# Self attention of a decoder: the subtracted maxima copied into the score banks by ScalarE, and the weighted sums issued in four pieces per group

## The chip, the cores and the metric

The kernel runs on one core of one Trainium2 chip. The metric is the device time of the whole program in microseconds (us), over several runs; the median is given. One further execution was recorded by the hardware profiler, and every row below is from that one. PE is TensorE's matmul, PEld its load of the stationary operand, DVE is VectorE, ACT is ScalarE, POOL is GpSimd.

## The reference, cut to what matters

The program is a two-layer decoder on `x` of shape (8, 512, 256). The change touches one of its six stages, the self attention of the second layer, which comes after a feed-forward stage and before a cross attention:

```
qkv = X @ W_qkv                              # X: layernorm of x; 16 heads of 64
scores = einsum('bqhd,bkhd->bhqk', q, k) / sqrt(64)
weights = softmax(scores, axis=-1)
attn = einsum('bhqk,bkhd->bqhd', weights, v)
x = x + attn.reshape(b, s, h * d) @ W_out
```

There are 8 batch elements of 512 tokens. All is float32.

## The kernel before, in words

Scores are held transposed, keys on the partitions and queries along the free axis, so that the product with V needs no transpose. Two heads (2 x 64 = 128 rows) make a **group**; a batch element has 8 groups, c = 0 to 7, and a group has 4 **chunks** of 128 keys, k = 0 to 3. For a chunk, "exact" (L1588, L1591) computes the two heads' scores, 128 keys x 512 queries each, into the two banks of the PSUM tensor ST. float32 precision is reached by splitting q and k into a high and a low part: three products per head (high-high, high-low, low-high), and in the kernel before a fourth (L1591) that multiplies a row of ones with `mrow`, the negated maximum of every query, and so subtracts the maximum from the scores. ScalarE then takes the exponential of both banks at once (L1649) into `PT`. There is one ST, so the next chunk's scores wait for this exponential.

The maxima come from a pass ahead of it. "max" (L1568) computes rough scores of one block of 128 queries, with queries on the partitions, into SM; VectorE reduces them (L1671) into `nmax`. When a group's four reductions are done, "mt" (L1575) transposes `nmax` with four small matmuls into one bank of W, and ScalarE copies that to `mrow` (L1644). `nmax` is 128 columns wide per block, with zeros where no maximum stands.

The other work of the stage: "q", "k", "v" and "norm" (L1535, L1546) are the projections and transposed activations, three groups and more ahead of their use. "av" (L1601) multiplies all four chunks of `PT` with V into OP, 16 instructions in one run; ScalarE copies the result out (L1653). "sum" (L1608) multiplies ones with `U`, the sum of a group's four chunks of `PT` that GpSimd makes (L1709, L1712), and so gives the softmax's denominators; VectorE takes their reciprocal (L1685) and scales the result (L1688). "out" (L1616) is the last projection.

Every engine walks the same list, which the function `plan` writes out by hand, and takes from it the steps that are its own, strictly in that order. A step that waits holds up everything behind it on its engine. In a middle group TensorE's order is: exact 0, max, q; exact 1, max, k; exact 2, max, sum (of the group before); exact 3, mt, v; av; max.

The steps q, k, v, norm, mt, sum and out share the three banks of W in rotation: each takes the bank that the third-last such step had, and waits (`free_bank`) until its reader has released it. ScalarE releases the banks of v and mt. VectorE releases the others, that of sum when the reciprocal ends. In a middle group the rotation before is q, k, sum, mt, v.

The last batch element has its own list, without the steps that prepare a next one. The rest run in a loop of seven passes.

## Time and profile before

| | |
|---|---|
| median of 3 runs | 3023.49 us (3019.45 to 3025.32) |
| the profiled execution: its own time | 3020.66 us |
| its span, first to last instruction | 3018.8 us |
| PE busy over the span | 91% |
| DVE, ACT, POOL busy over the span | 64%, 48%, 37% |

The span is the part of the profiled execution that the trace covers; 1.9 us lie around it. Busy shares are means over six stages with different limits. The self attention runs from about 1050 to 2196 us after the span's start, one batch element every 144.3 us.

### The profile page before, as it was taken

Reading aid. Unit: us, or ns where it says so; the run is one execution under the profiler, and the core shown is the slowest. Engines: PE = TensorE matmul, PEld = TensorE weight load, DVE = VectorE, ACT = ScalarE, POOL = GpSimd, SP = SyncE. Lnnn points to the kernel's source line nnn. Section 1 sums busy time; section 2 is a strip of 40 time slices with the busy share of each in tenths; the row PEclk is TensorE's granted clock in tenths of the full one; section 3 lists DMA queues with packets and bytes.
Section 4 is the critical chain, followed back from the end, with each engine's and each line's share of the span. In section 5 each row is a group of like instructions: output and inputs, shape, how many; then the busy total and the mean of one; then the engine's idle time right before and its main releaser. Section 6 shows DMA issues by size and latency. Waiting matters only on the chain. (4 is left out here: it accounts for less than half of the span.)

```text
span 3018.8 us, 49274 instructions
## 1 busy us (share of the span) xinstructions
PE 2760.4 (91%) x16604; PEld 1622.9 (54%) x16605; DVE 1922.6 (64%) x3109; ACT 1446.6 (48%) x2224; POOL 1103.7 (37%) x853
## 2 busy tenths in 40 slices
PE   7997899999868899999999999999889999966998
PEld 4774333333335555555555555555445555566997
DVE  5775666667668766657575757575645555474565
ACT  2342566666668743434343434343335555543333
POOL 3233332222037243434343434343443333153333
PEclk9998899999979999999999999999989999958999
DMA  5002222222111000000000000000043222146665
GB/s 159 0 0 74 53 58 56 57 57 52 33 56 43 1 1 1 0 0 0 0 0 0 0 0 0 0 0 0 1 110 79 71 67 71 45 113 232 214 218 194
DMA packets 102928, 159.71 MB, mean 53 GB/s; under 512 B 28349, under 2 KB 63432, under 8 KB 97160
## 3 DMA queue, kind: packets, MB, share of 16 engines
q1 hardware_dynamic: 97784, 147.88, 17.0%
q0 software_dynamic: 3408, 8.46, 0.8%
q10 hardware_dynamic: 1600, 1.61, 0.2%
q8 instruction: 79, 1.29, 0.2%
q14 instruction: 57, 0.47, 0.1%
HBM read 91.79 MB, written 14.96 MB: 35 GB/s over the span
## 5 line engine op out<-in xcount | busy, mean ns | idle before, releaser
L1671 DVE TENSOR_REDUCE self_nmax<-self_SM 128x2 f32<-128x1024 f32 x256 | 313.8, 1226 | 185.3 <-PE self_SM L1568 178.5
L522 DVE TENSOR_REDUCE cross_nmax<-cross_S 128x2 f32<-128x1024 f32 x256 | 311.7, 1224 | 153.3 <-PE cross_S L347 152.4
L1709 POOL TENSOR_TENSOR self_U<-self_PT 128x1024 f32<-128x1024 f32 x64 | 153.1, 2392 | 626.0 <-ACT self_PT L1649 626.0
L1649 ACT ACTIVATE self_PT<-self_ST 128x1024 f32<-128x1024 f32 x256 | 262.3, 1025 | 217.1 <-PE self_ST L1591 217.1
L1712 POOL TENSOR_TENSOR self_U<-self_U,self_PT 128x1024 f32<-128x1024 f32 x128 | 304.0, 2375 | 55.2 <-ACT self_PT L1649 50.7
L456 ACT ACTIVATE cross_PT<-cross_S 128x1024 f32<-128x1024 f32 x256 | 260.7, 1025 | 118.0 <-PE cross_S L358 117.1
L1186 DVE TENSOR_REDUCE cross_nmax<-cross_S 128x4 f32<-128x1024 f32 x128 | 156.7, 1224 | 143.3 <-PE cross_S L984 143.1
L1601 PE MATMUL self_OP<-self_PT,self_V 128*64 128x512 f32 x1024 | 233.8, 598 | 10.0 <-ACT self_PT L1649 10.0
L1685 DVE RECIPROCAL self_rcp<-self_W 128x512 f32<-128x512 f32 x64 | 214.1, 3345 | 8.4 <-PE self_W L1608 8.4
L1112 ACT ACTIVATE cross_PT<-cross_S 128x1024 f32<-128x1024 f32 x128 | 131.0, 1023 | 121.4 <-PE cross_S L1000 121.4
L377 PE MATMUL cross_W<-cross_PT,cross_V 128*32 128x512 f32 x1024 | 139.1, 618 | 8.0 <-DVE cross_rsin L554 8.0
L1601 PEld LDWEIGHTS self_OP<-self_PT,self_V 128*64 128x64 f32 x1024 | 69.5, 136 | 139.1 <-issue 132.8
L358 PEld LDWEIGHTS cross_S<-cross_qs,cross_ks 51*128 51x128 f32 x512 | 48.3, 186 | 169.9 <-issue 120.5
L617 POOL TENSOR_TENSOR cross_rows<-cross_rows,cross_cos 128x512 f32<-128x512 f32 x30 | 38.4, 1280 | 276.6 <-DVE cross_rsin L554 276.6
L1588 PE MATMUL self_ST<-self_q_hi,self_k_hi 64*128 64x512 f32 x512 | 123.0, 476 | 16.6 <-ACT self_PT L1649 15.4
L358 PE MATMUL cross_S<-cross_qs,cross_ks 51*128 51x512 f32 x512 | 129.4, 504 | 6.9 <-DMA cross_qs<-cross_mrow 3.3
L1653 ACT COPY self_Oraw<-self_OP 128x512 f32<-128x512 f32 x64 | 37.5, 587 | 197.2 <-PE self_OP L1601 197.2
L1568 PE MATMUL self_SM<-self_k_hi,self_q_hi 64*128 64x512 f32 x512 | 114.0, 440 | 19.2 <-DVE self_nmax L1671 19.2
L347 PE MATMUL cross_S<-cross_ks,cross_qs 49*128 49x512 f32 x512 | 109.3, 424 | 12.6 <-ACT cross_PT L456 11.1
L3100 PE MATMUL moe_TR<-moe_W,moe_hid_hi 128*128 x312 | 114.8, 406 | 0.0
L1616 PE MATMUL self_W<-self_wo,self_OT 128*128 128x256 f32 x512 | 112.5, 380 | 1.0 <-DVE self_OT L1688 1.0
L1588 PEld LDWEIGHTS self_ST<-self_q_hi,self_k_hi 64*128 64x128 f32 x512 | 47.8, 183 | 119.4 <-ACT self_PT L1649 70.1
(435 smaller groups left out, 6401.8 us busy)
## 6 DMA issues: line engine op xcount, KB each, us to landing
moe_staged<-in_L_ffn_W SPq DMA_DIRECT2D x36, 1024.0 KB, 5.9
cross_ks<-cross_parts SPq DMA_DIRECT2D x384, 64.0 KB, 2.2
cross_qs<-cross_parts SPq DMA_DIRECT2D x376, 64.0 KB, 2.3
all_x<-in_L_ffn_W SPq DMA_DIRECT2D x14, 1024.0 KB
all_x<-sorted_rows SPq DMA_DIRECT2D x83, 130.0 KB, 2.3
cross_cT<-in_ctx_T SPq DMA_DIRECT2D x16, 512.0 KB, 4.3
sorted_rows<-all_spare_row SPq DMA_DIRECT2D x1, 5460.0 KB, 23.8
all_x<-in_x SPq DMA_DIRECT2D x8, 512.0 KB, 6.1
```

What stands on the lines that cost most here:

```text
L358: m = pe.matmul(dst[:, r, :], ks[rows_r, p, k * P:(k + 1) * P], qs[rows_r, p, :], start=True, stop=True)
L377: m = pe.matmul(dst[32 * j:32 * j + 32, :], V[:, b % 2, k, 2 * p + r, :], PT[:, pt_slot[("exact", b, NT * p + k)], r, :], start=(k == 0), ...
L456: act.activation(PT[:, pt_slot[st], :, :], S[:, slot[st], :, :], ACT.Exp).then_inc(s_exped, 1)
L522: dve.tensor_reduce(nmax[:, g % 2, 0:R, n % PER_G], S[:, slot[st], :, :], AX.X, ALU.max, negate=True).then_inc(s_maxed, 1)
L1186: dve.tensor_reduce(nmax[:, g % 2, 0:R, n0:n0 + 2], S[:, slot[st], :, :].rearrange("p r (i c) -> p r i c", i=2), AX.X, ALU.max, negate=Tru ...
L1588: pe.matmul(ST[:, j, :], l[at, slot, at_k], r[at, slot, :], start=(t == 0), stop=False)
L1601: m = pe.matmul(OP[j * D:(j + 1) * D, :], V[:, k, 2 * n + j, :], PT[:, k, j, :], start=(k == 0), stop=(k == NT - 1), skip_group_check=True)
L1649: act.activation(PT[:, k, :, :], ST[:, :, :], ACT.Exp).then_inc(exped.sem, 1)
L1671: dve.tensor_reduce(nmax[:, i, 0:P:D], SM[:, :, :], AX.X, ALU.max, negate=True).then_inc(maxed.sem, 1)
L1685: dve.reciprocal(rcp[:, :], bank_of(order, st)).then_inc(done, 1)
L1709: pool.tensor_tensor(U[:, c % 2, :, :], PT[:, 0, :, :], PT[:, 1, :, :], ALU.add).then_inc(added.sem, 1)
L1712: pool.tensor_tensor(U[:, c % 2, :, :], U[:, c % 2, :, :], PT[:, k, :, :], ALU.add).then_inc(added.sem, 1)
```

## The change

In the score banks: the product of ones with `mrow` is gone. ScalarE writes the negated maxima into ST before the chunk's scores are computed, and the three remaining products of every chunk add onto them. For that "mt" becomes two steps per group, one for each head: four transposes of a maximum column that is broadcast along the free axis, so that the bank then holds the negated maxima of all 512 queries on every partition. ScalarE copies such a bank twice, into ST (for chunk 0 of the next group) and into a new SBUF tensor `least`. For chunks 1 to 3 it copies `least` to ST (128 x 1024) after the exponential of the chunk before. A new counter, `filled`, tells TensorE that the banks are ready. Two matmuls at the very start of the stage write ST once.

In the weighted sums: "av" becomes four steps of 4 instructions, one per chunk. The piece of chunk k - 1 comes after the other work behind exact k; the last piece of a group comes in the next group, behind exact 0 and q. Group 7 issues its last piece itself, before its own sum.

Two memsets by GpSimd in the stage before are gone.

```diff
@@ -1372,7 +1372,7 @@
         self.low = [s.sb(n, [P, KC, H * 64], F32R) for n in ("wq_lo", "wk_lo", "wv_lo")]
         self.wo = s.sb("wo", [P, H * 64 // P, C])
         self.hT_hi, self.hT_lo = s.sb("hT_hi", [P, KC, T], F32R), s.sb("hT_lo", [P, KC, T], F32R)
-        self.nmax, self.ones_r, self.ones = s.sb("nmax", [P, NT, P]), s.sb("ones_r", [P, P], F32R), s.sb("ones", [P, 64])
+        self.nmax, self.ones = s.sb("nmax", [P, NT, 2]), s.sb("ones", [P, 64])
         self.half, self.eps, self.minus = (s.sb(n, [P, NT]) for n in ("half", "eps", "minus"))
 
 
@@ -1406,6 +1406,9 @@
                 add("exact", c * NT + k, NC * NT)
                 if k < NT - 1:
                     add("max", (c + 1) * NT + k + 1, NC * NT)
+                else:
+                    for j in range(2):
+                        add("mt", (c + 1) * 2 + j, NC * 2)
                 if k == 0:
                     add("q", c + 2, NC)
                 elif k == 1:
@@ -1420,16 +1423,17 @@
                     if c:
                         add("sum", c - 1, NC)
                 else:
-                    add("mt", c + 1, NC)
                     if c < NT:
                         add("v", NT + c, HALF * NT)
                     if c == 5:
                         add("norm", KC + 1, KC)
                     if c >= 6:
                         add("v", HALF * NT + 2 * (c - 6), HALF * NT)
-            add("av", c, NC)
+                if k or c:
+                    add("av", c * NT + k - 1, NC * NT)
             add("max", (c + 2) * NT, NC * NT)
             if c == NC - 1:
+                add("av", NC * NT - 1, NC * NT)
                 add("sum", c, NC)
             if c >= 6:
                 add("v", HALF * NT + 2 * (c - 6) + 1, HALF * NT)
@@ -1446,7 +1450,7 @@
                "act": lambda kind: kind in RINGED and drained_by(kind) == "act",
                "dve": lambda kind: kind in RINGED and drained_by(kind) == "dve",
                "split": lambda kind: kind in ("q", "k", "norm")}
-    for kind in ("exact", "max", "av", "sum"):
+    for kind in ("exact", "max", "sum"):
         counted[kind] = lambda k, kind=kind: k == kind
 
     class Pass:
@@ -1471,10 +1475,10 @@
         s = Space(nc, ctx, "self1")
         h_tok = x_mem[:, 0:NT, :]
         (wq, wk, wv), (wq_lo, wk_lo, wv_lo), wo = buffers.high, buffers.low, buffers.wo
-        hT_hi, hT_lo, nmax, ones_r, ones = buffers.hT_hi, buffers.hT_lo, buffers.nmax, buffers.ones_r, buffers.ones
+        hT_hi, hT_lo, nmax, ones = buffers.hT_hi, buffers.hT_lo, buffers.nmax, buffers.ones
         half, eps, minus = buffers.half, buffers.eps, buffers.minus
         q_hi, q_lo, k_hi, k_lo = (s.sb(n, [P, SLOTS_QK, T], F32R) for n in ("q_hi", "q_lo", "k_hi", "k_lo"))
-        mrow = s.sb("mrow", [P, T], F32R)
+        least = s.sb("least", [P, 2, T])
         V = s.sb("V", [P, NT, H, D])
         PT = s.sb("PT", [P, NT, 2, T])
         U = s.sb("U", [P, 2, 2, T])
@@ -1496,7 +1500,8 @@
         split = loop("split", "split")
         scored, exped = loop("scored", "exact"), loop("exped", "exact")
         guarded, maxed = loop("guarded", "max"), loop("maxed", "max")
-        valued, lifted = loop("valued", "av"), loop("lifted", "av")
+        valued, lifted = Loop(s.sem("valued"), NC), Loop(s.sem("lifted"), NC)
+        filled = Loop(s.sem("filled"), NC * (NT + 1), 2)
         scaled = loop("scaled", "sum")
         added = Loop(s.sem("added"), 3 * NC)
         normed, s_stat, rooted = Loop(s.sem("normed"), NT), Loop(s.sem("stat"), 2 * NT), Loop(s.sem("rooted"), 4)
@@ -1536,7 +1541,7 @@
             return m
 
         def tensor_steps(pe, b, order):
-            n_exact = n_max = 0
+            n_max = 0
             for st in order.steps:
                 kind, n, rel = st
                 if kind == "norm":
@@ -1569,38 +1574,38 @@
                                       start=True, stop=True)
                     m.then_inc(guarded.sem, 1)
                 elif kind == "mt":
+                    c, j = n // 2, n % 2
                     dst = free_bank(pe, b, order, st)
-                    reach(pe, maxed, "max", b, order, ("max", n * NT + NT - 1, rel))
+                    if j == 0:
+                        reach(pe, maxed, "max", b, order, ("max", c * NT + NT - 1, rel))
                     for i in range(NT):
-                        m = pe.transpose(dst[:, i * P:(i + 1) * P], nmax[:, i, :], ident)
+                        m = pe.transpose(dst[:, i * P:(i + 1) * P], nmax[:, i, j:j + 1].to_broadcast([P, P]), ident)
                     m.then_inc(ring_full.sem, 1)
                 elif kind == "exact":
                     c, k = n // NT, n % NT
-                    exped.wait(pe, b, n_exact)
-                    n_exact += 1
+                    filled.wait(pe, b, (NT + 1) * c + k)
                     if k == 0:
                         reach(pe, drained["dve"], "dve", b, order, ("k", c, rel))
-                        reach(pe, drained["act"], "act", b, order, ("mt", c, rel))
                     slot, at_k = c % SLOTS_QK, slice(k * P, (k + 1) * P)
                     for t, (l, r) in enumerate(((k_hi, q_hi), (k_hi, q_lo), (k_lo, q_hi))):
                         for j in range(2):
                             at = slice(j * D, (j + 1) * D)
-                            pe.matmul(ST[:, j, :], l[at, slot, at_k], r[at, slot, :], start=(t == 0), stop=False)
-                    for j in range(2):
-                        at = slice(j * D, (j + 1) * D)
-                        m = pe.matmul(ST[:, j, :], ones_r[at, :], mrow[at, :], start=False, stop=True)
+                            m = pe.matmul(ST[:, j, :], l[at, slot, at_k], r[at, slot, :], start=False, stop=(t == 2),
+                                          skip_group_check=True)
                     m.then_inc(scored.sem, 1)
                 elif kind == "av":
-                    exped.wait(pe, b, NT * (n + 1))
-                    lifted.wait(pe, b, n)
-                    if n in (0, NC // 2):
-                        v = n // (NC // 2)
-                        reach(pe, drained["act"], "act", b, order, ("v", v * NT + NT - 1, rel))
-                    for k in range(NT):
-                        for j in range(2):
-                            m = pe.matmul(OP[j * D:(j + 1) * D, :], V[:, k, 2 * n + j, :], PT[:, k, j, :],
-                                          start=(k == 0), stop=(k == NT - 1), skip_group_check=True)
-                    m.then_inc(valued.sem, 1)
+                    c, k = n // NT, n % NT
+                    exped.wait(pe, b, n + 1)
+                    if k == 0:
+                        lifted.wait(pe, b, c)
+                        if c in (0, NC // 2):
+                            v = c // (NC // 2)
+                            reach(pe, drained["act"], "act", b, order, ("v", v * NT + NT - 1, rel))
+                    for j in range(2):
+                        m = pe.matmul(OP[j * D:(j + 1) * D, :], V[:, k, 2 * c + j, :], PT[:, k, j, :],
+                                      start=(k == 0), stop=(k == NT - 1), skip_group_check=True)
+                    if k == NT - 1:
+                        m.then_inc(valued.sem, 1)
                 elif kind == "sum":
                     dst = free_bank(pe, b, order, st)
                     added.wait(pe, b, 3 * (n + 1))
@@ -1641,16 +1646,26 @@
                     v, i = n // NT, n % NT
                     act.copy(V[:, i, v * 8:(v + 1) * 8, :], src.rearrange("p (h d) -> p h d", d=D)).then_inc(drained["act"].sem, 1)
                 elif kind == "mt":
-                    act.copy(mrow[:, :], src).then_inc(drained["act"].sem, 1)
+                    c, j = n // 2, n % 2
+                    exped.wait(act, b, 0 if order is first else NT * (NC if rel else c))
+                    act.copy(ST[:, j, :], src).then_inc(filled.sem, 1)
+                    filled.wait(act, b, 0 if order is first else (NT + 1) * ((NC if rel else c) - 1) + NT - 1)
+                    act.copy(least[:, j, :], src).then_inc(drained["act"].sem, 1)
                 elif kind == "exact":
                     c, k = n // NT, n % NT
                     scored.wait(act, b, n + 1)
                     added.wait(act, b, 3 * (c - 1) + max(k, 1))
                     act.activation(PT[:, k, :, :], ST[:, :, :], ACT.Exp).then_inc(exped.sem, 1)
-                elif kind == "av":
-                    valued.wait(act, b, n + 1)
-                    scaled.wait(act, b, n - 1)
-                    act.copy(Oraw[:, n % 2, :], OP[:, :]).then_inc(lifted.sem, 1)
+                    if k < NT - 1:
+                        if k == 0:
+                            reach(act, drained["act"], "act", b, order, ("mt", 2 * c + 1, rel))
+                        exped.wait(act, b, n + 1)
+                        act.copy(ST[:, :, :], least[:, :, :]).then_inc(filled.sem, 1)
+                elif kind == "av" and n % NT == NT - 1:
+                    c = n // NT
+                    valued.wait(act, b, c + 1)
+                    scaled.wait(act, b, c - 1)
+                    act.copy(Oraw[:, c % 2, :], OP[:, :]).then_inc(lifted.sem, 1)
 
         def vector_steps(dve, b, order):
             n_max = 0
@@ -1668,7 +1683,7 @@
                     c, i = n // NT, n % NT
                     n_max += 1
                     guarded.wait(dve, b, n_max)
-                    dve.tensor_reduce(nmax[:, i, 0:P:D], SM[:, :, :], AX.X, ALU.max, negate=True).then_inc(maxed.sem, 1)
+                    dve.tensor_reduce(nmax[:, i, :], SM[:, :, :], AX.X, ALU.max, negate=True).then_inc(maxed.sem, 1)
                 elif kind in ("q", "k", "norm"):
                     split.wait(dve, b, order.nth["split"][st])
                     src = bank_of(order, st)
@@ -1714,6 +1729,8 @@
         with nc.Block() as block:
             @block.tensor
             def _(pe):
+                for j in range(2):
+                    pe.matmul(ST[:, j, :], wq[:, 0, 0:P], hT_hi[:, 0, :], start=True, stop=True)
                 tensor_steps(pe, None, first)
                 for counter in (ring_full, scored, guarded, valued):
                     counter.credit(pe)
@@ -1724,7 +1741,7 @@
             @block.scalar
             def _(act):
                 scalar_steps(act, None, first)
-                for counter in (drained["act"], split, exped, lifted, normed):
+                for counter in (drained["act"], split, exped, filled, lifted, normed):
                     counter.credit(act)
                 with act.Fori(0, B - 1) as b:
                     scalar_steps(act, b, whole)
@@ -2595,8 +2612,6 @@
                 bound_x(1)
                 for tensor, value in ((following.half, -0.5), (following.eps, EPS), (following.minus, -1.0), (following.ones, 1.0)):
                     pool.memset(tensor[:, :], value).then_inc(s_fset, 1)
-                pool.memset(following.ones_r[:, :].bitcast(F32), 1.0).then_inc(s_fset, 1)
-                pool.memset(following.nmax[:, :, :], 0.0).then_inc(s_fset, 1)
                 normalise(1, range(NT))
                 for t in range(TILES + 1):
                     b, i = t // NT, t % NT
```

## Rows read from the trace of the kernel before

In a row of a stretch stand: start and end, its length, the busy time and count of PE, PEld, DVE, ACT and POOL, the granted clock of PE, the DMA share and GB/s.

**Rows 1.** Stretches: groups 0, 1, 4, 5, 6, 7 and one batch element.

```profile
1484.45:1500.49 16.04, 14.43 (x80) 8.16 (x80) 5.48 (x6) 7.67 (x10) 7.14 (x3) 1.00 0.00 0
1500.49:1516.35 15.86, 15.47 (x84) 8.30 (x82) 11.35 (x8) 6.93 (x10) 7.17 (x3) 1.00 0.00 0
...
1548.13:1563.48 15.35, 14.17 (x78) 7.46 (x76) 11.39 (x8) 6.35 (x9) 7.11 (x3) 1.00 0.00 0
1563.48:1579.29 15.81, 15.17 (x86) 8.12 (x84) 12.27 (x10) 7.30 (x11) 7.12 (x3) 1.00 0.00 0
1579.29:1596.87 17.58, 17.19 (x90) 9.19 (x87) 12.57 (x9) 7.30 (x10) 7.15 (x3) 1.00 0.00 0
1596.87:1628.73 31.86, 31.86 (x157) 21.56 (x156) 16.57 (x13) 8.10 (x11) 7.15 (x3) 1.00 0.00 0
1484.45:1628.73 144.28, 139.29 (x729) 79.34 (x728) 94.28 (x78) 59.37 (x79) 58.68 (x28) 1.00 0.00 0
```

**Rows 2.** Timeline of PE, group 1: start us, duration, operation, count [idle before].

```profile
1500.15 0.51 PE L1568 MATMUL self_SM<-self_k_hi,self_q_hi 64*128 64x512 f32 x2
1500.49 0.40 PE L1588 MATMUL self_ST<-self_q_hi,self_k_hi 64*128 64x512 f32 x2
...
1501.18 0.40 PE L1591 MATMUL self_ST<-self_mrow,self_ones_r 64*128 64x512 f32 x2
1501.97 0.50 PE L1568 MATMUL self_SM<-self_k_hi,self_q_hi 64*128 64x512 f32 x2 [0.39 <-DVE self_nmax L1671]
1502.40 0.50 PE L1535 MATMUL self_W<-self_hT_hi,self_wq 128*128 128x512 f32 x1
...
1503.98 0.51 PE L1588 MATMUL self_ST<-self_q_hi,self_k_hi 64*128 64x512 f32 x2
...
1508.30 1.08 PE L1608 MATMUL self_W<-self_U,self_ones 128*64 128x512 f32 x4
1509.33 0.50 PE L1588 MATMUL self_ST<-self_q_hi,self_k_hi 64*128 64x512 f32 x2
...
1510.46 0.66 PE L1575 MATMUL self_W<-all_ident,self_nmax 128*128 128x128 f32 x4
1510.87 0.47 PE L1535 MATMUL self_W<-self_wv,self_hT_hi 128*128 128x512 f32 x1
...
1512.43 3.65 PE L1601 MATMUL self_OP<-self_PT,self_V 128*64 128x512 f32 x16
1516.02 0.50 PE L1568 MATMUL self_SM<-self_k_hi,self_q_hi 64*128 64x512 f32 x2
```

**Rows 3.** Timeline of DVE, group 1: the last reduction, the reciprocal, the scaling.

```profile
1508.41 1.23 DVE L1671 TENSOR_REDUCE self_nmax<-self_SM 128x2 f32<-128x1024 f32 x1
1509.56 3.35 DVE L1685 RECIPROCAL self_rcp<-self_W 128x512 f32<-128x512 f32 x1
1513.03 1.81 DVE L1688 TENSOR_TENSOR self_OT<-self_Oraw,self_rcp 128x512 f32<-128x512 f32 x1
```

**Rows 4.** Timeline of ACT, end of group 1: an exponential and the copy behind it.

```profile
1510.65 1.03 ACT L1649 ACTIVATE self_PT<-self_ST 128x1024 f32<-128x1024 f32 x1 [1.37 <-PE self_ST L1591]
1511.58 0.58 ACT L1644 CAST self_mrow<-self_W 128x512 fp32r<-128x512 f32 x1
```

**Rows 5.** Timeline of PE, last group: a chunk's last product, the next chunk's first.

```profile
2170.45 0.40 PE L1591 MATMUL self_ST<-self_mrow,self_ones_r 64*128 64x512 f32 x2
2171.96 0.50 PE L1588 MATMUL self_ST<-self_q_hi,self_k_hi 64*128 64x512 f32 x2 [1.11 <-ACT self_PT L1649]
```

**Rows 6.** Timeline of DVE, group 5: norm's low part, ahead of the reciprocal.

```profile
1572.81 0.69 DVE L1681 TENSOR_TENSOR self_hT_lo<-self_W,self_hT_hi 128x512 fp32r<-128x512 f32 x1
```

**Rows 7.** Timeline of PE: the first matmul after the stage's end.

```profile
2203.65 1.97 PE L1062 MATMUL cross_W<-all_ident,all_x 128*128 128x128 f32 x8 [7.28 <-ACT all_x L1129]
```

**Rows 8.** Stretches behind that matmul; columns as in rows 1.

```profile
2206.00:2208.00 2.00, 2.00 (x4) 0.70 (x3) 0.00 (x0) 0.24 (x1) 0.00 (x0) 0.50 0.90 314
...
2210.00:2214.00 4.00, 4.00 (x13) 2.20 (x12) 2.33 (x4) 0.69 (x1) 2.26 (x2) 1.00 0.19 47
```

## The prediction

> **What bounds the kernel now.** I read the page's shares first: PE is busy 91% of the span, no other engine above 64%. Then the stretches of the stage [rows 1]: a batch element takes 144.28 us, PE is busy in 139.29 of them at a granted clock of 1.00 (2.4 GHz), and ACT works 59. TensorE's own list therefore sets the pace. Its waits in the timeline of a middle group are one, of 0.39, on a reduction [rows 2]. So an edit counts by what it does to TensorE's start-to-start times, and by the waits it creates there.
>
> Those times come from the timeline of PE [rows 2]. One exact after max takes 0.34 to the next start in front and 0.23 for each further pair of products: the fourth product starts at 1501.18, 0.69 after the first (0.23 a pair). max to exact is 0.34. q from its start to exact is 1.58 (1502.40 to 1503.98). sum, 4 instructions, is 1.03 from start to next start. exact 3 to mt is 1.13, mt to v 0.41, v to av 1.56, and av, 16 instructions, 3.59 (1512.43 to 1516.02). The wait on the reduction makes two maxes stand at least 1.82 apart (1500.15 to 1501.97).
>
> **Work of TensorE, per group.** The product of ones goes: 4 x 0.23 = -0.92. The second mt: +0.41. av in four pieces: a piece has the shape of sum (64 stationary columns, 512 moving ones, 4 instructions), so each costs up to 1.03, four 4.12 in place of 3.59. Behind sum the piece finds the array in the same form; four bare instructions are (3.59 - 0.17) / 4 = 0.86, with 0.17 the excess of sum over this, so one piece is about 0.86 and the others 1.03. I take 1.03 for the piece and 0.86 for the sum ahead of it: 3.95, or +0.36. Both maxes around exact 0 still stand 1.82 apart, so there exact's 0.23 turns into wait: +0.23. Together -0.92 + 0.41 + 0.36 + 0.23 = +0.08: the saving is already spent. Counted alone, the product of ones would be worth 256 x 0.23 = 59 us; the other three terms take that back.
>
> **The cycle of ST.** From a chunk's last product to the next chunk's first it now takes 1.51 (2170.45 to 2171.96) where only the exponential stands between [rows 5]. The fill comes on top. No row shows ScalarE writing PSUM. The nearest are the exponential of as many elements, 1.03, and the 512-wide copy, 0.58 [rows 4]. Below: 2 x 0.58 less a fixed part, about 0.9; above: I allow 1.4. I take 1.02 plus 0.05 for waiting on its own exponential, since back-to-back instructions overlap by 0.10 [rows 4] and this one cannot. So 2.58 to 2.60 from last product to next first. The Trainium skill (ScalarE: Activation LUTs, "Step-by-step: what each stage is for") holds that ScalarE writes PSUM faster than SBUF; by that the fill would be at the lower end and the sum some 2 us smaller, and no row here shows it.
>
> **The bank rotation.** The rotation of W becomes q, k, sum, mt, mt, v. The third-last step before v is now sum (it was k), and sum's bank is freed only when the reciprocal ends. The reciprocal starts 1.26 after sum and takes 3.35 [rows 2, 3]. So v can't start before sum + 4.66, whereas before it started at sum + 2.57 while the reciprocal ran. This is what decides.
>
> **A middle group walked through** (exact 0 at 0, in us). max 1.48, q 1.91, av piece 3.49, exact 1 at 4.52 (ST ready at 3.1, hidden). max 5.32, k 5.65, av piece 7.24, exact 2 at 8.27 (ST ready 7.7, hidden). max 9.07, sum 9.40, av piece 10.26, done 11.29. ST is ready at 8.84 + 2.60 = 11.44: exact 3 waits 0.15. mt 12.34, second mt 12.75, v could go at 13.16, but its bank is free at 9.40 + 4.66 = 14.06: 0.90 of wait. v to 15.62, av piece to 16.65, max to 16.99. ScalarE's four copies after exact 3 (ST, least, ST, least) have ST ready by 15.1: hidden. GpSimd's three sums need 7.2 of 17: hidden, and so is the copy out of OP. Group: 16.99 against 15.86 [rows 1], +1.13. A fill slower by 0.7 changes little here, since v's wait takes it up.
>
> The page on TensorE of the Trainium skill (TensorE: Matmul & The Clock Gate, "Part 4: PE-mode transpose") gives about 275 ns for a transpose in a kernel. The timeline has four of them in 0.41 from start to start, so they overlap; four of 275 ns would be 1.1, and the sum about 30 us larger.
>
> **The other groups, same method.** Group 0 has no sum before its v and no av piece behind exact 0. Exact 1 waits for the exponential and the fill (0.74 later than before, as the fill is longer than the product of ones it replaces), exact 3 for the fill: 15.99 against 16.04, -0.05. Group 4 has no v: the next exact 0 waits for the second mt's fill, 15.1 against 15.35, -0.2. Group 5: its second norm takes the bank of sum. There the reciprocal is later too, for VectorE must first make norm's low part, 0.69 [rows 6], and that waits for ScalarE's high part, now queued behind exponential and fill (until 12.5 after exact 0). Also the reduction of group 4's last max waits for the scaling, up to 1.81 long [rows 3] and behind the late reciprocal, +0.47. Reciprocal 13.1 to 16.45, norm at 16.5 (waits 2.4), group 18.46 against 15.81: +2.65. Group 6: as a middle one, 19.07 against 17.58, +1.5. Group 7 has five av pieces and v behind a reciprocal, 33.55 against 31.86, +1.7; out hides its last reciprocal as before. Sum: -0.05 + 3 x 1.1 - 0.2 + 2.65 + 1.5 + 1.7 = +8.9 per batch element, 62 for seven. The last element, with no norm and no v at its end, I put at +5. The second mt and its copies at the entry: +0.4. The two removed memsets lie on GpSimd in a stage where PE doesn't wait for them: 0.
>
> **Sum.** 3020.66 + 62 + 5 + 0.4 = 3088. The median shown is 2.8 above the profiled execution, so 3090 on that scale.
>
> **Rivals.**
> *The bank of sum costs nothing* (I misread the rotation, or the reciprocal is out of the way earlier). Five groups lose their 0.90, group 5 its 2.4: 6.9 x 7 and 2.7, or 51 less, 3039. For it: nothing but possible error; the reciprocal has never been under 3.3 in a row. 6%.
> *Faster*: v does not wait, and a piece of av costs the bare 0.86. Then a group is -0.92 + 0.41 - 0.15 + 0.23 = -0.43, 64 of them -27: 2996. It decides only if both hold: without the bank's wait the break-even is a piece of 0.97, with it 0.65, under the four bare instructions. Against it: the 1.03 of sum in the same place. 3%.
> *The clock falls* in the new gaps. After PE stood idle for 7.28 us its next matmuls ran at 0.50 (1.2 GHz), until some point from 2208 to 2210, and at 1.00 later [rows 7, 8]; after gaps of 1.1 it stayed at 1.00. Group 5's wait of 2.4 lies between. 5 us at half speed lose 2.5, seven times: 17 more, 3107. 8%. The Trainium skill's page on TensorE ("HAM oscillation") also has idle gaps between bursts bring the slower clock.
> *The fill is dear* (1.4): groups 0, 4 and 7 lose 3 x 0.4, others 0.2: 12 more, 3102. 10%.
>
> **Chances and range.** Forecast 70%, its own range 3075 to 3103 (a piece of 0.86 everywhere takes 3 x 0.17 per v group off, about 15; fill at either end -2 to +12). Dear fill 10%, clock 8%, free bank 6%, faster 3%, other 3%. I leave out free bank and faster below and take in the clock above: 3055 to 3115. Faster 4%, same (within 0.2%, about 6 us, which is what a measurement of this kernel can tell from none) 2%, slower 94%.
>
> **What would show it.** In the profile after: v (L1535 after the second mt) waits about 0.9 for the DVE reciprocal in groups 1 to 3, 6, 7, norm in group 5 about 2.4; a middle group lasts 17.0; L1601 runs as pieces of 4 at 1.03; exact 3 waits 0.1 to 0.2 for ScalarE; the granted clock stays 1.00. Wrong would be: no wait on the reciprocal, a fill far from 1.02, or ScalarE named as the releaser in most waits.

## The result, and the profile after

| | before | after |
|---|---|---|
| median of 4 runs each | 3022.14 us (3019.45 to 3025.32) | 3115.02 us (3111.2 to 3119.66) |
| profiled execution, its span | 3020.66, 3018.8 | 3111.2, 3109.4 |
| mean of the seven batch elements in the loop | 144.28 | 157.02 |

The changed kernel is slower by 3.1% (ratio 1.0308, 95% interval 1.029 to 1.0326). The forecast was 3090 with a range of 3055 to 3115: the sign was right, the size 25 us too small, and the median lies 0.02 us above the upper end. Nearly all of it lies in the loop: 7 x (157.02 - 144.28) = 89.2 of the 90.5 us between the two profiled executions. The last element is 6.1 longer, and what lies ahead of and behind the stage 4.8 shorter.

The page of the changed kernel, its busy times and two groups:

```profile
PE 2772.9 (89%) x16350; PEld 1593.5 (51%) x16351; DVE 1935.0 (62%) x3109; ACT 1740.4 (56%) x2608; POOL 1105.8 (36%) x851
...
L1605 PE MATMUL self_OP<-self_PT,self_V 128*64 128x512 f32 x1024 | 277.7, 621 | 0.1
...
L1663 ACT COPY self_ST<-self_least 128x1024 f32<-128x1024 f32 x192 | 195.4, 1018 | 9.6
```

The fill takes 1018 ns (I had taken 1.02 us). ScalarE is at 56%, far from a bound. PE's share fell from 91% to 89%, so it now waits more.

The stretches of the changed kernel, groups 0 to 7 of the fourth batch element and the element as a whole (columns as in [rows 1]):

```profile
1519.20:1535.34 16.14, 13.35 (x71) 7.37 (x72) 5.49 (x6) 11.93 (x15) 7.11 (x3) 1.00 0.00 1
1535.34:1552.30 16.96, 15.58 (x80) 7.75 (x78) 12.02 (x8) 11.64 (x16) 7.13 (x3) 1.00 0.00 0
1552.30:1571.07 18.77, 15.59 (x80) 7.77 (x78) 12.79 (x16) 11.52 (x15) 8.66 (x7) 1.00 0.00 0
1571.07:1588.00 16.93, 15.57 (x80) 7.77 (x78) 10.24 (x8) 13.31 (x19) 7.32 (x3) 1.00 0.00 0
1588.00:1603.17 15.17, 14.09 (x75) 6.62 (x72) 10.73 (x8) 10.47 (x14) 6.38 (x4) 1.00 0.00 0
1603.17:1622.46 19.29, 15.62 (x80) 7.88 (x82) 13.26 (x11) 12.49 (x17) 7.92 (x4) 0.97 0.00 0
1622.46:1642.99 20.53, 19.75 (x87) 9.95 (x83) 13.32 (x9) 11.49 (x15) 7.13 (x3) 0.86 0.00 0
1642.99:1676.50 33.51, 32.76 (x158) 21.45 (x157) 17.71 (x13) 13.10 (x18) 7.14 (x3) 1.00 0.00 1
1519.20:1676.50 157.30, 142.33 (x698) 76.58 (x697) 95.55 (x78) 95.94 (x127) 58.78 (x28) 0.98 0.00 0
```

Three things are to be seen. Groups 1, 3, 4 and 7 are within 0.07 of what the prediction walked through (16.99, 16.99, 15.1, 33.55; "the walk" from here on). Group 2 has the same PE work as group 1 (15.59 busy against 15.58) and yet takes 1.81 longer: a wait that the walk does not have. In groups 5 and 6 the granted clock stands at 0.97 and 0.86, where it was 1.00 before [rows 1].

The PE timeline of group 1 (columns as in [rows 2]) shows the wait that was forecast:

```profile
1544.70 1.08 PE L1613 MATMUL self_W<-self_U,self_ones 128*64 128x512 f32 x4
1545.61 1.03 PE L1605 MATMUL self_OP<-self_PT,self_V 128*64 128x512 f32 x4
1546.71 0.50 PE L1593 MATMUL self_ST<-self_q_hi,self_k_hi 64*128 64x512 f32 x2
1547.60 1.09 PE L1582 MATMUL self_W<-all_ident,self_nmax 128*128 128x128 f32 x8
1549.36 0.50 PE L1540 MATMUL self_W<-self_wv,self_hT_hi 128*128 128x512 f32 x1 [0.67 <-DVE self_rcp L1700]
1550.96 1.08 PE L1605 MATMUL self_OP<-self_PT,self_V 128*64 128x512 f32 x4
```

The time from sum to v is 4.66 (1544.70 to 1549.36), to the hundredth what the walk had: the reciprocal starts 1.26 after sum, takes 3.35, and v starts 0.05 behind its end. (The prediction's text names only the first two, 4.61.) sum and the piece behind it take 0.91 and 1.10 to the next start, together 2.01 (1.89 was assumed, and 0.15 of wait). The idle time in brackets, 0.67, looks less than the 0.90 forecast, but it is counted from an end that the profile models. From start to start the eight transposes take 0.84 where nothing holds v up (group 0, 1531.59 to 1532.43) and 1.76 here: the wait costs 0.92. In group 2 the same wait has 2.49 of idle. The DVE timeline of that group says why:

```profile
1562.91 1.40 DVE L1677 BATCH_NORM_STATS2 self_stats<-all_x 128x6 f32 x4
1564.46 0.38 DVE L1681 BATCH_NORM_AGGREGATE self_mv<-self_stats 128x2 f32<-128x6 f32 x4 [0.16 <-DVE self_stats L1677]
1564.76 3.33 DVE L1700 RECIPROCAL self_rcp<-self_W 128x512 f32<-128x512 f32 x1
```

Eight small instructions of the layernorm statistics ("stat" in the list, for the next batch element) stand ahead of the reciprocal: 1.85 us from 1562.91 to 1564.76. They stood there before as well, as the same view of the kernel before shows:

```profile
1525.43 1.40 DVE L1662 BATCH_NORM_STATS2 self_stats<-all_x 128x6 f32 x4
1526.98 0.38 DVE L1666 BATCH_NORM_AGGREGATE self_mv<-self_stats 128x2 f32<-128x6 f32 x4 [0.16 <-DVE self_stats L1662]
1527.28 3.32 DVE L1685 RECIPROCAL self_rcp<-self_W 128x512 f32<-128x512 f32 x1
```

There the group's sum starts at 1524.17, so its reciprocal comes 3.11 behind it and not 1.26 as in group 1. That cost TensorE nothing while v took the bank of k. Since sum's bank is now the one that v needs, every microsecond ahead of the reciprocal is one of TensorE's.

The releasers of PE's waits in the changed kernel (total us, times, longest):

```profile
PE self_W L1540 <- DVE self_rcp L1700: 37.1, 38, 2.5
PE self_SM L1573 <- DVE self_nmax L1686: 36.1, 44, 1.6
...
PE self_ST L1593 <- ACT self_ST L1663: 24.4, 20, 1.8
...
PE self_W L1551 <- DVE self_rcp L1700: 14.5, 7, 2.1
```

The first and the last line are the bank's wait, 51.6 in all; the wait on the reductions was there before, at 19.2.

And the clock, in the PE timeline at the end of group 5 and the start of group 6:

```profile
1620.09 0.66 PE L1551 MATMUL self_W<-all_ident,all_x 128*128 128x128 f32 x4 [2.06 <-DVE self_rcp L1700]
...
1625.31 0.63 PE L1540 MATMUL self_W<-self_hT_lo,self_wq 128*128 128x512 f32 x1
1625.73 0.63 PE L1540 MATMUL self_W<-self_hT_hi,self_wq_lo 128*128 128x512 f32 x1
```

Products that follow each other at 0.23 elsewhere are 0.42 apart here. The time at half clock can be read from the stretches as 2 x (1 - granted clock) x length, summed over the groups: 3.4 to 7.0 us in each of the seven batch elements, in groups 5 and 6 and in three of the seven also in group 2 (which is then 20.1 to 20.2 long).

### The profile page after: what moved, and what is told of

Its sections match the earlier page's. It is cut to its first block and busy times, and to the rows that moved or that the text cites. A ratio compares the mean times of both kernels' runs of the same rounds, so it can differ in the third digit from the quotient of the medians.

```text
span 3109.4 us, 49675 instructions
## 1 busy us (share of the span) xinstructions
PE 2772.9 (89%) x16350; PEld 1593.5 (51%) x16351; DVE 1935.0 (62%) x3109; ACT 1740.4 (56%) x2608; POOL 1105.8 (36%) x851
## 3 DMA queue, kind: packets, MB, share of 16 engines
q10 hardware_dynamic: 1600, 1.61, 0.2%
## 5 line engine op out<-in xcount | busy, mean ns | idle before, releaser
L1605 PE MATMUL self_OP<-self_PT,self_V 128*64 128x512 f32 x1024 | 277.7, 621 | 0.1
L1186 DVE TENSOR_REDUCE cross_nmax<-cross_S 128x4 f32<-128x1024 f32 x128 | 156.8, 1225 | 141.7 <-PE cross_S L984 141.5
L1663 ACT COPY self_ST<-self_least 128x1024 f32<-128x1024 f32 x192 | 195.4, 1018 | 9.6
L1112 ACT ACTIVATE cross_PT<-cross_S 128x1024 f32<-128x1024 f32 x128 | 131.1, 1024 | 119.7 <-PE cross_S L1000 119.7
L1593 PE MATMUL self_ST<-self_q_hi,self_k_hi 64*128 64x512 f32 x512 | 125.4, 486 | 33.8 <-ACT self_ST L1663 24.4
L1703 DVE TENSOR_TENSOR self_OT<-self_Oraw,self_rcp 128x512 f32<-128x512 f32 x64 | 118.8, 1856 | 6.5
```

The source lines that it names most:

```text
L1186: dve.tensor_reduce(nmax[:, g % 2, 0:R, n0:n0 + 2], S[:, slot[st], :, :].rearrange("p r (i c) -> p r i c", i=2), AX.X, ALU.max, negate=Tru ...
L1593: m = pe.matmul(ST[:, j, :], l[at, slot, at_k], r[at, slot, :], start=False, stop=(t == 2), skip_group_check=True)
L1605: m = pe.matmul(OP[j * D:(j + 1) * D, :], V[:, k, 2 * c + j, :], PT[:, k, j, :], start=(k == 0), stop=(k == NT - 1), skip_group_check=True)
L1663: act.copy(ST[:, :, :], least[:, :, :]).then_inc(filled.sem, 1)
```

## The experiments

Each ratio is against the kernel before, run on the same chip beside it. Where a difference is small, the stage itself says more than the whole time. In the sixteen profiled executions its first scores start between 1048.3 and 1056.2 us, and what lies behind it takes 819 to 827, with no order by kernel. So the eight batch elements ("the stage" below) are compared as well: 1144.7 us in the kernel before, 1240.1 in the changed one.

| kernel | median us | ratio (95% interval) |
|---|---|---|
| e1, pieces alone | 3105.25 | 1.0277 (1.0258 to 1.0296) |
| e2, maxima alone | 3202.37 | 1.0605 (1.0585 to 1.0625) |
| e3, v ahead of mt | 3080.02 | 1.019 (1.0173 to 1.0207) |
| e4, every fill twice | 3188.84 | 1.0555 (1.0536 to 1.0574) |
| e5, stat behind sum | 3110.44 | 1.0295 (1.0268 to 1.0323) |
| e6, group 5's norms behind av | 3131.34 | 1.0363 (1.0332 to 1.0393) |
| e7, pieces, scaling later | 3021.57 | 0.9993 (0.9981 to 1.0004) |
| e8, all moves | 3005.72 | 0.9943 (0.9921 to 0.9965) |
| e9, scaling later alone | 3098.32 | 1.0245 (1.0228 to 1.0262) |
| e10, before with max ahead of av | 2996.66 | 0.991 (0.9893 to 0.9926) |
| e11, e7 with max ahead | 3004.49 | 0.9928 (0.9911 to 0.9945) |
| e12, e8 with v in group 0 | 2993.32 | 0.9894 (0.9877 to 0.9911) |
| e13, PE kept busy in two waits | 3113.85 | 1.0312 (1.0294 to 1.033) |
| e14, three moves | 3050.47 | 1.0099 (1.0082 to 1.0117) |

### e1 and e2: the two halves of the change alone

e1 is the kernel before, with its product of ones, and the four pieces; e2 is the changed kernel with the weighted sums in one run again. Of e1's edit only the list is shown; the rest is as in the change.

```diff
+                if k or c:
+                    add("av", c * NT + k - 1, NC * NT)
-            add("av", c, NC)
             add("max", (c + 2) * NT, NC * NT)
             if c == NC - 1:
+                add("av", NC * NT - 1, NC * NT)
                 add("sum", c, NC)
...
```

> The kernel before with the weighted sums in four pieces and nothing else. Theory (the pieces cost TensorE its change of form, 32 pieces of 1.03 in place of 8 runs of 3.59, and give back waits for the exponential that they now cover): per batch element 31.8 against 28.7, so +3.1, less the waits covered in groups 0 (0.96), 4 (0.80) and 5 (0.25): +1.1, about +8 in all, 3030 us (3022 to 3040). Rival (the pieces are what made the changed kernel slower): +50 or more, above 3070.

> The changed kernel with the weighted sum again as one run per group behind v. Theory (the fill by ScalarE lengthens the cycle of the score banks to 2.6 us from last product to next, and only the pieces cover it): exact 2 waits 0.45, exact 3 about 1.0, group 0 more; a middle group about 17.9 us against 16.96 in the changed kernel; in all about 3175 us (3150 to 3200). Rival (the pieces are a cost in this kernel too): below 3115.

e2 came close to its expectation, 3202 for 3175, 2 above its range: the fill, no longer covered by a piece of av, is exposed, and PE waits 97.6 us for it in all. e1 did not: 3105, where 3030 was expected. The DVE and POOL timelines of e1, group 1, at its end:

```profile
1541.37 3.35 DVE L1690 RECIPROCAL self_rcp<-self_W 128x512 f32<-128x512 f32 x1
1544.84 2.58 DVE L1693 TENSOR_TENSOR self_OT<-self_Oraw,self_rcp 128x512 f32<-128x512 f32 x1
1547.34 1.21 DVE L1676 TENSOR_REDUCE self_nmax<-self_SM 128x2 f32<-128x1024 f32 x1
```

```profile
1544.49 2.38 POOL L1717 TENSOR_TENSOR self_U<-self_U,self_PT 128x1024 f32<-128x1024 f32 x1 [0.87 <-ACT self_PT L1653]
```

With av spread out, the group's last max comes about two pieces earlier, and VectorE reaches its reduction only after reciprocal and scaling. The scaling itself is stretched from 0.69 to 2.58 while GpSimd adds. The next max then waits, and e1's list of waits has it in one line:

```profile
PE self_SM L1570 <- DVE self_nmax L1676: 75.0, 48, 2.6
```

These 75 us, where the kernel before had 19.2, and the falls of the clock behind them are most of the loss. So the two halves, +82 and +179, do not add up to the +93 of both. The pieces cover the fill. And the group's last max comes later behind the sum than in e1, so that its reduction is less in the way: the wait is 0.63 behind groups 1 and 2 of the changed kernel, and 1.07 and 2.0 behind groups 1 and 2 of e1. The second mt is enough for that, since the wait is still 0.62 behind group 1 of e3 below, where v waits for nothing.

### e3: v ahead of mt

```diff
-                else:
-                    for j in range(2):
-                        add("mt", (c + 1) * 2 + j, NC * 2)
...
                     if c < NT:
                         add("v", NT + c, HALF * NT)
-                    if c == 5:
-                        add("norm", KC + 1, KC)
                     if c >= 6:
                         add("v", HALF * NT + 2 * (c - 6), HALF * NT)
+                    for j in range(2):
+                        add("mt", (c + 1) * 2 + j, NC * 2)
+                    if c == 5:
+                        add("norm", KC + 1, KC)
```

v then takes the bank of k, and mt that of sum only one step later. This is the direct test of the bank rotation.

> The changed kernel with v ahead of the two mt steps, so that the second mt, not v, takes the bank of sum, 4.9 us after sum. Theory (the bank that the reciprocal holds for 4.66 us is what v waits for): the waits of 0.67 in groups 1, 3, 6 and 7 vanish, that of group 2 shrinks from 2.5 to 1.6; 3.6 per batch element, 27 in all: 3088 us (3080 to 3100). Rival (VectorE or ScalarE is the bound and the wait only moves to another step): 3105 to 3120.

3080.02, where 3088 was expected. The line of v's wait on the reciprocal is gone from the list of waits. The norm's 14.5 remains, and a new line has the second mt wait for the reciprocal, 9.9 in all: 1.4 in group 2 of each element, where stat delays it. Groups 1 and 3 are 16.05 and 16.3 for 16.96 and 16.94. By this run the bank of sum in front of v is worth 35 us of the loss. An element without a fall of the clock takes 150.7 here and 154.95 in the changed kernel, which is 30 us for seven, and half of what is left of the 35 is fewer falls. The 27 expected were added up from idle times of 0.67; group 1 became shorter by 0.90, the wait from start to start.

### e4: every fill twice

```diff
                         act.copy(ST[:, :, :], least[:, :, :]).then_inc(filled.sem, 1)
+                        filled.wait(act, b, 2 * NT * c + 2 * k + 1)
+                        act.copy(ST[:, :, :], least[:, :, :]).then_inc(filled.sem, 1)
```

> The changed kernel with every fill of ST from least made twice, one after the other: 192 more copies of 1.02 us and a wait of 0.05 on ScalarE. Theory (the fill is mostly hidden; exact 2 has 0.5 of slack, exact 3 none, and the wait on the reciprocal takes up 0.7): a middle group +0.9, group 0 +2.4 to 3, others 1 to 1.5, about 10 per batch element, 80 in all: 3195 us (3165 to 3225). Rival 1 (the fill is fully exposed, ScalarE bounds the stage): 3 x 1.07 per group, 64 groups, +205: 3320. Rival 2 (the fill is free): 3115.

3188.84 (3195 was expected), or 74 more than the changed kernel, for 192 fills of 1.02 (196 us): between free and fully exposed. Middle groups grow from 16.96 to 17.53, and the wait for ST from 24.4 to 122.9 in total. The single fill is just covered in middle groups, as the walk had it, with little to spare.

### e5, e6 and e9: the three instructions in VectorE's way

e5 moves stat behind sum; e6 moves both norms of group 5 behind the last piece of av in that group; e9 leaves TensorE's list alone and lets VectorE scale one group later.

```diff
-                    if c == 2:
-                        add("stat", 1, 1)
...
                     if c:
                         add("sum", c - 1, NC)
+                    if c == 2:
+                        add("stat", 1, 1)
```

```diff
-                    if c == 5:
-                        add("norm", KC, KC)
...
-                    if c == 5:
-                        add("norm", KC + 1, KC)
...
+            if c == 5:
+                for n in range(KC):
+                    add("norm", KC + n, KC)
             add("max", (c + 2) * NT, NC * NT)
```

```diff
                 if k == 0:
                     add("q", c + 2, NC)
+                    if c >= 2:
+                        add("scale", c - 2, NC)
...
-                    drained["dve"].wait(dve, b, order.nth["dve"][st])
+                elif kind == "scale":
+                    drained["dve"].wait(dve, b, order.nth["dve"][("sum", n, rel)])
                     lifted.wait(dve, b, n + 1)
```

> The changed kernel with VectorE's statistics of the next batch element (group 2, 1.85 us) behind the sum step in place of ahead of it. Theory (they hold back group 2's reciprocal, and with it the bank that v waits for): group 2 from 18.76 to 16.96, seven times 12.6, and the clock falls that followed its wait of 2.5 us in three of seven batch elements, 4 more: 3098 us (3093 to 3104). Rival (something else in group 2): 3112 to 3118.

> The changed kernel with both norm steps of group 5 behind its third av piece, so that neither waits for the reciprocal. Theory (the wait of 2.1 us there costs itself, and once more by the clock that falls behind it, some 1.5 us a time): groups 5 and 6 together from 38.3 to 39.9 down to 35 to 37, seven times 2.5 to 3, 3095 us (3088 to 3102), and a granted clock of 1.00 in group 6. Rival (the clock falls for another reason): groups 5 and 6 lose only the wait and the clock in group 6 stays under 1.00: above 3102.

> The changed kernel with only the scaling of the output moved to the next group's chunk 0. Theory (here, unlike in the kernel with the pieces alone, v's wait on the reciprocal holds the group's last max back far enough that the scaling is done, except behind group 4, which has no v): only group 5's first wait of 1.6 shrinks to about 0.6, seven times 1.0, and a part of the clock falls: 3105 us (3095 to 3112). Rival (the scaling is what costs in this kernel too): below 3060.

e5 gave 3110.44, 5 less than the changed kernel in place of the 17 expected, and the intervals of the two overlap. But e5's stage started 5.8 later and what lies behind it took 3.2 longer, which the edit does not touch; its loop is 11.4 shorter than the changed kernel's. The stretches of e5, groups 2 and 5 of one element, show why it worked and why it did not bring all that was expected:

```profile
1554.72:1571.65 16.93, 15.56 (x80) 7.75 (x78) 11.93 (x16) 11.51 (x15) 4.95 (x3) 1.00 0.00 0
...
1603.80:1624.44 20.64, 16.97 (x80) 8.73 (x82) 13.24 (x11) 12.48 (x17) 7.93 (x4) 0.90 0.00 0
```

Group 2 fell to 16.93 in all seven elements, as it should; group 5 has more time at the lower clock. One of e5's seven elements, the one without a fall, is at 153.04 against the walk's 153.2; their mean is 155.4. So stat is the missing step of the walk. The 4 us expected on top from fewer falls did not come: the clock costs 2.4 per element here, and 2.1 in the changed kernel.

e6 missed: 3131.34, slower by 16 than the changed kernel where 20 less was expected. Groups 5 and 6 take 18.3 and 21.8 in most elements, with a clock of 0.91 and 0.92. The norms' low parts now stood, with the scaling, ahead of the next reduction; the bank's wait had turned into waits of up to 2.4 for the reduction. In the stage the clock fell 23 times, against 10 in the changed kernel.

e9 gave 3098.32 (3105 was expected, below 3060 if the scaling were the cost here too). Group 5 shrinks from 18.87 at full clock to 17.24: its first max had waited 1.61 for group 4's last reduction, which stood behind the scaling, and that wait is gone. The norm's wait of 2.1 stays. Three of its seven elements have no fall, at 153.2 to 153.3.

### e7: pieces alone, scaling later

The edit of e9 on e1.

> The kernel before with the weighted sums in four pieces, as e1, and VectorE's scaling of the output (L1688) moved from right behind the reciprocal to the next group's chunk 0. Theory (in e1 the max at the group's end comes two pieces nearer to the sum, while the reciprocal and the scaling, stretched to 2.5 us while GpSimd adds, still hold VectorE; the next max waits 1.07 to 2.0 and the clock falls behind the longer ones): the wait shrinks to 0.4, the granted clock is 1.00 throughout, 3030 us (3022 to 3045). Rival (the pieces themselves cost 80 us on TensorE): above 3080.

3021.57, the same as the kernel before within its interval, and just under the 3022 to 3045 expected. The DVE timeline has the scaling at its short length, in GpSimd's pause, and the stretch of one element is at 144.58 with a clock of 1.00:

```profile
1540.28 0.68 DVE L1698 TENSOR_TENSOR self_OT<-self_Oraw,self_rcp 128x512 f32<-128x512 f32 x1
```

```profile
1488.62:1633.20 144.58, 141.32 (x730) 77.51 (x730) 86.05 (x78) 59.55 (x79) 58.61 (x28) 1.00 0.00 0
```

The 84 us of e1 were thus the place of one VectorE instruction. The pieces' own TensorE work costs a middle group some 0.3 (16.16 against 15.9), and group 0, which has only three of them, gives 1.56 back (14.48 against 16.04).

### e8, e10, e11 and e12: is there a version that beats both?

e8 is the changed kernel with the moves of e3, e5, e6 and e9, and the group's last max ahead of the piece of av. e10 is the kernel before with that last move alone, e11 is e7 with it, and e12 is e8 with group 0's v put behind its q, where the wait for ST was. Two cuts of these edits follow: the early max, as e10 has it, and e12's move of v.

```diff
+            add("max", (c + 2) * NT, NC * NT)
             add("av", c, NC)
-            add("max", (c + 2) * NT, NC * NT)
```

```diff
                     add("q", c + 2, NC)
+                    if c == 0:
+                        add("v", NT, HALF * NT)
...
-                    if c < NT:
+                    if 0 < c < NT:
                         add("v", NT + c, HALF * NT)
```

> The changed kernel with all of the orders mended at once: v ahead of the mt steps, the statistics behind sum, the norm steps of group 5 behind the av piece, the scaling in the next group, and the max of the group's end ahead of the av piece in chunk 3, so that the two maxes around exact 0 are more than 1.82 us apart. Theory (TensorE's list is the bound once no bank and no reduction is waited for, and the product of ones then counts): a middle group 16.06 less 0.68 of wait, 15.4 against 15.87, a batch element 141, in all 2995 us (2980 to 3015). Rival (the saving stays spent on the pieces and the second mt): 3020 to 3040.

> The kernel before with the max of the group's end ahead of av, and nothing else. Theory (that max and the next one then stand further apart than 1.82 us): the wait of 0.39 and a change of form go, a group 15.4 to 15.5 against 15.87, 48 times 0.4: 3003 us (2998 to 3010). Rival (the reduction, now nearer to the scaling, holds up the next max): 3020 or more.

> e7 (four pieces, scaling late, product of ones kept) with the group's last max ahead of the piece in chunk 3. It is e8 without the maxima written by ScalarE, and e10 with pieces. Theory (the maxima by ScalarE save 0.92 per group and cost 0.41 for the second mt, and cost waits in group 0; the pieces cost 0.36 and cover waits): a middle group 15.8, 3000 us (2993 to 3010). Rival (the maxima by ScalarE lose even in the mended order): below 2990.

> e8 with the v of group 0 moved from chunk 3 to behind q in chunk 0, into the wait for table load, exponential and fill. Theory (that wait of 1.8 is covered by v's 1.55, the clock doesn't fall behind it, and 0.6 of wait appears at the group's end): 1.6 less per batch element, 2995 us (2988 to 3003). Rival (the wait only moves to chunk 3): 3003 to 3010.

e12 has 2993.32 and e10 2996.66, and their intervals overlap (e10 came out 1 us under the range expected of it, e12 within its own). In the stage e10 is the shorter one, 1118.7 against 1121.1. e8 has 3005.72 for 2995: in three of its seven elements the clock fell behind group 0's wait of 1.8 for ST, the wait that e12 then filled. One element of e10 and one of e12:

```profile
1475.05:1615.99 140.94, 138.87 (x729) 79.39 (x728) 93.80 (x78) 59.40 (x79) 58.74 (x28) 1.00 0.00 0
```

```profile
1474.11:1615.22 141.11, 137.43 (x697) 75.75 (x697) 85.11 (x78) 95.15 (x127) 58.49 (x28) 1.00 0.00 0
```

Both run at a clock of 1.00 throughout. In e12 PE is busy for 1.44 less per element, but idle for 1.61 more (3.68 against 2.07), so the whole change is worth nothing that these runs can tell, once the order suits it. e11 parts its halves. With the early max the pieces cost 8 us (e11's 3004.49 against e10's 2996.66; 6.8 in the stage, no fall in either). Filling the maxima as well, against e11, gives nothing in e8 (3005.72; its elements without a fall are at 142.0 to 142.1, e11's at 142.3), and 11 us in e12, of which only 4.3 lie in the stage, where v fills the wait that the fill makes in group 0. Moving one line of the old list (e10) brings 28 us, 26 of them in the stage: the reduction of the group's last max now runs under av, and PE is busy all through a middle group (15.43 of 15.43), where the two maxes had a wait of 0.39 between them [rows 2].

### e13 and e14: the clock

Still open was whether the falls of the clock can be stopped by keeping PE busy in the waits. e13 adds idle products into SM, whose results nobody reads, in group 2 and group 5, where the waits on the reciprocal were:

```diff
+                if order is whole and st[:2] in (("v", NT + 2), ("norm", KC - 1)):
+                    for _ in range(9 if kind == "v" else 7):
+                        pe.matmul(SM[:, 0, :], wq[:, 0, 0:P], wk[:, 0, 0:512], start=True, stop=True)
```

e14 is the changed kernel with the moves of e3, e5 and e9, whose sum was worked out from the stretches of those runs.

> The changed kernel with idle work for TensorE, whose results nobody reads, put into its two longest waits for the reciprocal: 9 products of 128x128 by 512 ahead of group 2's v (2.1 us into a wait of 2.5) and 7 ahead of group 5's second norm (1.6 into a wait of 2.1), written to SM. Theory (the clock falls because TensorE stands idle in those waits, and the slow stretch behind them is a cost of its own): the granted clock stays 1.00 in groups 2 and 6, group 2 always 18.8, some 1.5 us less per batch element, 3104 us (3097 to 3110). Rival (the falls have another cause, or cost nothing that TensorE's later waits don't take up): 3112 to 3120.

> The changed kernel with e3's, e5's and e9's orders together: v ahead of the mt steps, statistics behind sum, scaling late. Theory (the effects add up, since each takes away one wait on VectorE): groups 16.2, 16.05, 16.05, 16.3, 15.0, 17.1, 17.8, 32.7, a batch element 147.1, clock 1.00, 3046 us (3038 to 3058), so still 0.8% above the kernel before, for the pieces, the second mt, the wait between maxes and the fills of group 0. Rival (a wait taken away comes back elsewhere): above 3060.

e13: 3113.85, the same as the changed kernel, where 3104 was expected; its rival (3112 to 3120) came true. Group 2 (first row) keeps its 18.7 with a wait of 0.4 where 2.49 was, and now never sees a fall; group 6 (second) runs at 1.00 too; one whole element (third) is free of falls:

```profile
1241.79:1260.52 18.73, 17.62 (x89) 9.36 (x87) 12.82 (x16) 11.52 (x15) 8.68 (x7) 1.00 0.00 0
...
1311.53:1330.17 18.64, 17.28 (x86) 8.70 (x82) 13.40 (x10) 11.51 (x15) 7.13 (x3) 1.00 0.00 0
...
1208.69:1363.66 154.97, 143.13 (x714) 77.88 (x713) 95.61 (x78) 95.93 (x127) 58.83 (x28) 1.00 0.00 0
```

Two of the seven elements are like this one (154.93 and 154.97). In the other five the clock fell at waits that were left open: group 0, which waits 1.76 for the fill, went from 16.14 to 17.65 in four of them, and group 5, whose first max still waits 1.59 for the reduction, from 18.87 to values of 20.3 to 21.8 in three. The mean is 156.8, against 157.02. So no fall began behind a filled wait, and falls came behind others.

e14: 3050.47, where 3046 (3038 to 3058) was expected. An element without a fall takes 147.34 (147.1 forecast), the mean is 148.95: the moves add up, and the clock costs 1.6 per element here (falls in groups 0, 5 and 6).

## Why the prediction was right, and where it was wrong

**Right.** The saving on TensorE is spent: the product of ones goes, and the second mt and the pieces take its place. PE is busy for 139.3 in the elements of e9 without a fall, which have TensorE's list of the changed kernel, against 139.29 before; the 142.33 shown above has the lower clock in it. The rotation of W is what decides: sum to v 4.66, and e3, which moves only that, gains 35 us. Groups 1 and 3 are 16.95 for 16.99, group 7 33.51 for 33.55, the fill 1.018 for 1.02, a chunk's last product to the next one's first 2.56 (1544.15 to 1546.71) for 2.58 to 2.60. The piece ahead of exact 3 takes 1.09 to 1.18 to the next start, and 0.96 in e1, where no fill stands ahead: exact 3 waits 0.13 to 0.22, where 0.15 was forecast. Three pieces at 1.01, that one at 0.96 and sum at 0.91 make 4.90 for the 4.62 of av and sum before, +0.28 where +0.36 was taken. The fill stays hidden in middle groups but for that, and e4 shows how narrowly. The last element is 6.1 longer, for 5 and 0.4 at the entry.

The Trainium skill gives a transpose, in bf16, about 275 ns in a kernel (TensorE: Matmul & The Clock Gate, "Part 4: PE-mode transpose"); eight one after the other would be 2.2 us by an estimate from that figure. The eight of group 0 take 0.84 from start to next start (1531.59 to 1532.43), in float32; the measurement decides. The Trainium skill also has ScalarE write PSUM faster than SBUF (ScalarE: Activation LUTs, "Step-by-step: what each stage is for"). The 128x512 copy takes 588 ns into ST, in PSUM, and 597 into `least`, in SBUF: the direction agrees, and at 1.5% it decides nothing.

**Wrong, first: a step is missing in "A middle group walked through".** The walk treats groups 1 to 3 alike ("3 x 1.1"), and names nothing ahead of the reciprocal but in group 5. In group 2, stat stands there, as it did in the kernel before: 18.76 instead of 16.99, 1.8 a time, 12 us for seven. Shown by e5, whose group 2 is 16.93. The other groups without a fall miss by little, and that they cancel is luck: group 5 18.87 for 18.46, group 6 18.6 for 19.07, group 0 16.14 for 15.99. In group 5 the wait on the reduction behind the scaling was too small in the sum: its first max starts 2.55 after exact 0 (1603.17 to 1605.72) where the walk of a middle group has 1.48, so 1.07 and not 0.47 more. An element without a fall is 154.95 (e13, whose added products replace waits; the groups without a fall of the changed kernel add up to the same), for 153.2 forecast. (That the "3 x 1.1" is 1.13 rounded down is worth 0.6 us in all.)

**Wrong, second: "the clock falls" was a rival at 8%, and it happened.** The forecast's own line was that the granted clock stays at 1.00. 157.02 - 154.95 = 2.07 per element, 14.5 for seven; the rival's price was 17. I had placed it behind group 5's wait only. It began behind a wait of group 5 in all seven elements, in some of them running on into group 6, and behind group 2's wait in three. The sum then closes: 12 + 14.5 in the loop and 1 in the last element, less the 4.8 ahead of and behind the stage, which is scatter and here was luck, make 22.7 of the 23.2 between 3111.2 and 3088. The remaining 2 up to 25 lie in the difference of median and profiled execution and in rounding. The Trainium skill (TensorE: Matmul & The Clock Gate, "HAM oscillation") has idle gaps between bursts bring the slower clock. The traces agree in direction: the clock was at 0.50 behind the waits listed under "Open".

The two together are why the forecast failed: each alone (3102 or 3105) lies well inside the range.

**What the forecast did not ask.** It costed the pieces as TensorE work only. e1 and e7 show that their real price lies on VectorE, where the same pieces cost 82 us or none by where the scaling stands. In the changed kernel this was in part included (the +0.47 in group 5), in part covered; e9 shows 17 us of it left.

**Open.** Not every long wait is followed by a fall. In the changed kernel's loop the clock fell behind 3 of the 7 waits of 2.5 us (group 2), 5 of the 7 of 2.1 and 2 of the 7 of 1.6 (both in group 5), and behind none of the 7 of 1.8 (group 0), while in e13 it fell behind 4 of the 7 in that place. A fall that is stopped at one place (e5, e13) shows up at another. What selects them is not settled by these runs. Nor did a run part e8's gain over e14 between the norms and the early max.

## What to carry to other kernels

When an edit adds a step to a ring of buffers, look up for every user which step it now inherits its buffer from, and then walk the releasing engine's own list for all that stands ahead of the release, small instructions too, group by group and not for a typical one. A saving on the busiest engine counts only if the waits around it go as well: here one moved line without any change of work gave 28 us, about as much as the whole mended redesign (32). Take what a wait costs from start to start, since the idle time in the profile is counted from modelled ends (0.67 for 0.92 here). Waits of the lengths seen here (1.6 us and more) in a dense stream of products can cost more than their length, since the clock may fall behind them; price that together with each new wait, and not as a case apart.

## What the runs showed of the hardware that was not expected

- The granted clock fell to 0.50 (1.2 GHz) behind single waits in a stream that is otherwise some 90% busy; starts were then 0.42 instead of 0.23 apart, 2.1 us lost per batch element on average. In the sixteen kernels' traces each of the 121 falls between the stage's first scores and its last began at the end of a wait of 1.5 to 2.8 us or shortly behind it. The kernels whose repeated waits in it were at most 1.2 us (before, e7, e10, e11, e12) ran in it at 1.00 throughout; waits of 1.4 us (e3, seven times) had no fall behind them either.
- A scaling of 128x512 on VectorE, with both operands in SBUF, takes 0.68 to 0.69 us when GpSimd is idle and up to 2.85 while GpSimd adds (2.38 a time). The Trainium skill (SBUF — State Buffer, "Who interferes with whom") says that a VectorE instruction with two SBUF inputs contends with a GpSimd instruction that reads SBUF; the traces agree, with a factor of up to 4.
- Sixteen instructions of av in one run take 3.59 us to the next start [rows 2]. In four pieces of four they take 3.99 (e1: 1.01 three times and 0.96), and 4.1 to 4.2 in the changed kernel, where the last figure has exact 3's wait in it. The piece of 0.96 stands behind sum, which has its form, the others behind products of another, and sum itself, right ahead of a piece, fell from 1.03 to 0.91. That the change of form is the reason is argued from these rows, not tested.
